# A fourth buffer for the one-hots of a cell group, and building them three groups ahead

## The reference, cut to what matters

```
h = relu(layernorm(x));  x = x + L0(h)   # h @ W1 + b1, then four gated aggregations over the edges
h = relu(layernorm(x));  x = x + L1(h)   # h @ W.T + bias, where W[src, dst] += edge_weight
h = relu(layernorm(x));  x = x + L2(h)   # graph convolution over the edges, normalised by degree
h = relu(layernorm(x));  x = x + L3(h)   # attention over the edges
```

## Time and profile before

| what | us |
|---|---|
| median of 3 runs (lowest, highest) | 993.5 (992.0, 993.78) |
| the profiled execution, its own time | 993.59 |
| span of the profile | 991.7 |
| PE busy | 969.9 (98%) |
| DVE busy | 674.9 (68%) |
| ACT busy | 443.1 (45%) |
| longest time that PE idles between 30 and 118 of the span | 2.30 |

### The profile page before, as it was taken

The page is one execution under the profiler, slowest core; times in us unless marked ns, Lnnn a source line. Parts: engine busy times, 40 slices in busy tenths (PEclk is TensorE's granted clock), DMA queues, the critical chain, the costliest instruction groups (busy, mean ns, idle before and its releaser), DMA issues.

```text
span 991.7 us, 14256 instructions
## 1 busy us (share of the span) xinstructions
PE 969.9 (98%) x5170; PEld 805.5 (81%) x5170; DVE 674.9 (68%) x1223; ACT 443.1 (45%) x662; POOL 140.0 (14%) x191
## 2 busy tenths in 40 slices
PE   5999999999999999999999999999999999999997
PEld 4788878888888888888888888888888888888885
DVE  7887798789788779468874115233346564988886
ACT  5689864544554547223335446002012322445543
POOL 3022510000000001223331000010100000333331
PEclk9999999999999999999999999999999999999999
DMA  7256490000000005543421040732231130101223
GB/s 253 90 187 227 123 272 1 1 22 0 0 21 0 0 0 117 98 147 127 138 96 65 1 171 14 282 113 101 85 128 69 69 122 1 44 22 63 85 85 123
DMA packets 25892, 88.28 MB, mean 89 GB/s; under 512 B 3370, under 2 KB 3370, under 8 KB 25696
## 3 DMA queue, kind: packets, MB, share of 16 engines
q1 hardware_dynamic: 14960, 52.82, 15.1%
q0 software_dynamic: 10880, 34.74, 11.4%
HBM read 59.23 MB, written 33.56 MB: 94 GB/s over the span
## 4 chain that ended last, share of the span: by engine, by line
PE 90%; DVE 5%; ACT 2%; DMA 1%; issue 1%; ACTq 0%; DVEq 0%
PE ps L611 21%; PE ps L2205 11%; PE ps L2179 11%; PE ps L2099 9%; PE ps L2100 9%; PE ps L2101 9%; PE ps L2155 5%; PE ps L2151 5%; PE ps L594 2%; DMA xin<-in_x 1%; PE ps L2022 1%; PE ps L2024 1%; PE ps L2023 1%; PE ps L1949 1%; PE ps L1965 1%
## 5 line engine op out<-in xcount | busy, mean ns | idle before, releaser
L2099 PE MATMUL ps<-g_hi,mask_hi 128*128 128x512 f32 x400 | 157.4, 394 | 2.1 <-DVE mask_lo L1571 2.1
L2101 PE MATMUL ps<-g_hi,mask_lo 128*128 128x512 f32 x400 | 155.8, 390 | 0.0
L2100 PE MATMUL ps<-g_lo,mask_hi 128*128 128x512 f32 x400 | 155.7, 389 | 0.0
L1114 ACT ACTIVATE mask<-ps,v 128x640 f32<-128x640 f32 x80 | 63.5, 793 | 111.3 <-PE ps L2101 52.9
L2205 PE MATMUL ps<-y_all,att_hi 128*128 128x512 f32 x400 | 110.0, 393 | 1.4 <-DVE att_lo L1820 1.4
L2099 PEld LDWEIGHTS ps<-g_hi,mask_hi 128*128 128x128 f32 x400 | 75.1, 188 | 20.5 <-DVE mask_lo L1571 3.3
L2101 PEld LDWEIGHTS ps<-g_hi,mask_lo 128*128 128x128 f32 x400 | 75.1, 188 | 16.0
L2205 PEld LDWEIGHTS ps<-y_all,att_hi 128*128 128x128 f32 x400 | 74.0, 188 | 17.3 <-DVE att_lo L1820 1.6
L2100 PEld LDWEIGHTS ps<-g_lo,mask_hi 128*128 128x128 f32 x400 | 75.1, 188 | 15.0
L611 PE MATMUL ps<-w,hT_hi 128*128 128x512 f32 x320 | 86.6, 392 | 0.0
L577 ACT ACTIVATE hT_hi<-ps 128x1024 fp32r<-128x1024 f32 x30 | 30.8, 1026 | 122.3 <-PE ps L594 122.1
(11 more groups left out here) (221 smaller groups left out, 1932.5 us busy)
## 6 DMA issues: line engine op xcount, KB each, us to landing
xin<-x_after SPq DMA_DIRECT2D x20, 512.0 KB, 3.3
xres<-x_after POOLq DMA_DIRECT2D x20, 512.0 KB, 3.6
x_after<-xres POOLq DMA_DIRECT2D x20, 512.0 KB, 2.9
w_raw<-in_L_gnn_W SPq DMA_DIRECT2D x8, 1024.0 KB, 10.8
x_after<-g POOLq DMA_DIRECT2D x20, 256.0 KB, 7.1
xres<-x_after SPq DMA_DIRECT2D x10, 512.0 KB, 3.3
xin<-in_x SPq DMA_DIRECT2D x9, 512.0 KB, 3.4
out_x<-xres SPq DMA_DIRECT2D x9, 512.0 KB, 2.6
```

The lines of the kernel that those rows point to most:

```text
L1114: nc.scalar.activation(mask[k][:, :], U_ALL, ACT.Tanh, bias=v[:, s:s + 1]).then_inc(tanh_ready, 1)
L2099: nc.tensor.matmul(SUMS[dd], mask_hi[k][:, cols], g_hi[:, s, :], start=(s == 0), stop=False)
L2100: nc.tensor.matmul(SUMS[dd], mask_hi[k][:, cols], g_lo[:, s, :], start=False, stop=False)
L2101: last = nc.tensor.matmul(SUMS[dd], mask_lo[k][:, cols], g_hi[:, s, :], start=False, stop=(s == T - 1))
```

## The change

Two constants change and two tiles are added: `RING` goes from 3 to 4 and `LEAD` from 2 to 3. The fourth pair, `left_last` and `right_last`, lies at 20 and 40 KiB of the region that holds the split first weights, in the gaps in front of `w1_hi` (24 to 40 KiB) and of `w1_lo` (44 to 60 KiB). No other tile moves.

```diff
-RING = 3
+RING = 4
...
-LEAD = 2
+LEAD = 3
...
-    left = [build(f"left{k}", [P, PER_GROUP, P], BF16) for k in range(RING)]
-    right = [build(f"right{k}", [P, PER_GROUP, CELLS + 3 * WCELLS], BF16) for k in range(RING)]
+    left = [build(f"left{k}", [P, PER_GROUP, P], BF16) for k in range(RING - 1)]
+    left += [at("left_last", [P, PER_GROUP, P], BF16, R_Y + 20 * KIB)]
+    right = [build(f"right{k}", [P, PER_GROUP, CELLS + 3 * WCELLS], BF16) for k in range(RING - 1)]
+    right += [at("right_last", [P, PER_GROUP, CELLS + 3 * WCELLS], BF16, R_Y + 40 * KIB)]
```

## The result

The changed kernel takes 994.89 us (median of 11 runs, 994.22 to 996.22), the kernel before 993.5 (11 runs, 992.0 to 994.36). The ratio is 1.0018, 95% interval 1.001 to 1.0026. Timed again beside the kernel before, it takes 995.27 against 993.11, ratio 1.0023 (1.0014 to 1.0032). It is slower by 1.4 to 2.2 us; 2.7 were forecast. One execution of a later experiment, lead1_copies_first, took 5575.49 us for a reason that stays open; it counts in that kernel's median of seven and not in its ratio.

The account below looks back on a forecast made before the run. PE, busy 98%, was taken as the bound, so only its early idle time or clock could matter. 993.59 + 2.65 (1.65 + 1.75 - 0.75) = 996.24, median 0.09 below: 996.2 us; own range 995.4 to 997.0, wider range 994.2 to 998.0.

Parts of the forecast that it names:

- What ends the hole: PE's 2.46 us hole before group 3, tile 2: ended by ACT's late copies of group 2, not by one-hot builds.
- The sum of 2.65: Delay of tile 4's ReLU and PE's group 3: + 1.65 `ew_ids` wait + 1.75 extra build - 0.75 old wait.
- the wait for `ew_ids`: DVE at the start: group 0, now before tile 3's statistics, must wait for `ew_ids`; + 1.65 us.
- the old wait for hT_hi: DVE before hT_lo of tile 2: its former wait for hT_hi disappears; - 0.75 us.
- The steady state: After the start, DVE's waits stay as they are; everything is moved by 2.65 us and nothing shrinks.
- POOL's scale: POOL's six instructions between variance and bias, partly beside group 1's build: 0 to about 1 us on the bias, 0 taken.
- The prediction's last sign: PE's idle time in 31.8 to 50 us grows by about 2.6 us: 1.45 opening, 0.8 group 1 and bias, 0.4 hole.
- The clock: PE's 3.42 us half-clock stretch behind the hole: same single stretch assumed, no difference; could vanish (-1.71) or come twice (+1.71).
- half clock missed after: Rival: most runs after miss PE's half-clock stretch, 993.5 + 2.65 - 1.71 = 994.4 us; chance 0.14.
- The faster rival: PE starves for one-hots before group 3; building further ahead wins 4.17 us, giving 989.3; chance 0.08.

Follow-up runs that it names:

- lead1_copies_first: Kernel before with three places, LEAD 1 instead of 2, and in tile 4 ACT copies group 10 before the ReLU of tile 6 and the bias; 990.21 us, ratio 0.997.
- before_again: The kernel before, unchanged, timed once more with its own trace; 993.19 us, ratio 0.9998.
- after_again: The changed kernel, unchanged, timed once more in the same rounds as the kernel before; 995.27 us, ratio 1.0023.
- lead1: Kernel before with three places and LEAD 1 instead of 2; 990.78 us, ratio 0.9976.
- stats_first: Kernel before (three places, lead two) with the statistics of tile 4 moved in front of the builds of groups 2 and 3 on DVE; 990.21 us, ratio 0.9972.

## Why the prediction was right

**What ends the hole.** Right. The chain builds, statistics, ReLU, bias, copies, group 3 is shown from both sides: one build more in front of the statistics costs 1.76 us, one less gives 1.65, and moving the statistics alone removes the hole with later one-hots.

**The sum of 2.65.** Right: 13.69 - 11.04 = 2.65 in both pairs of traces. Its terms are of another size with another start, though. In the pair with the same start the wait for `ew_ids` is 2.40, not 1.65, and the old wait for hT_hi 1.48, not 0.75. Both end behind the same step on ACT, so their difference holds while each of them moves: 2.40 + 1.75 - 1.48 = 2.67.

**The steady state.** Right: from the opening of tile 3 to the first matmul of the gates (line 2099) PE takes 77.45 us in before_again and 77.36 in after_again.

**POOL's scale.** I left 0 to about 1 us open and took 0. It is the upper end. The bias came 37.03 - 33.45 = 3.58 us after the variance started, against 2.59. POOL's timeline shows where:

```profile
33.69 0.70 POOL L553 TENSOR_TENSOR rough<-variance,minus_half 128x2 f32<-128x2 f32 x1 [17.47 <-DVE variance L533]
34.47 0.19 POOL L555 TENSOR_TENSOR square<-rough 128x2 f32<-128x2 f32 x1
34.74 0.44 POOL L557 TENSOR_TENSOR square<-square,variance 128x2 f32<-128x2 f32 x1
35.27 0.65 POOL L559 TENSOR_SCALAR step<-square 128x2 f32<-128x2 f32 x1
36.00 0.61 POOL L561 TENSOR_TENSOR scale<-rough,step 128x2 f32<-128x2 f32 x1
```

The first two run beside DVE's hT_lo, the next three beside the build that begins at 34.72, and take 0.44, 0.65 and 0.61, where the second took 0.19 and where POOL in the kernel before took 0.20, 0.19 and 0.20 for the same three. That the builds on DVE are what slows POOL is read from this coincidence and not tested. It costs nothing in the end, since group 3 comes later for another reason; but it turns hole into earlier waits. The hole is 1.87 us in the trace after, not 2.88. The prediction's last sign, PE idling about 2.6 us more before tile 3, was too high: the page of stretches gives 3.90 us after, against 1.76 in before_again and 2.30 in the first trace, so 2.14 and 1.60 more. And the growth lies in front of tile 2, the bias and group 1, not in the hole. The steps themselves are 2.64 later; the rest is, by my estimate, how the page counts: a product matmul is busy for 0.39 us where the next can start after 0.23, so each of the three waits more hides some 0.16 us.

**The clock.** This term was mis-sized. I took one stretch at half rate in both kernels, no difference, and judged that most executions pay it. The changed kernel paid it in 0 of 22 runs. The kernel before paid it in its first trace, but only in 24 of the 88 runs that later studies give a clock for. That explains a part of what is missing. In the study of after_again the runs of the kernel before without the stretch have a median of 992.77, and 995.27 - 992.77 = 2.50, near the 2.65; those with it have 993.57. For the first comparison, 1.39 us apart, the clocks of the runs before are not known, so there it stays open. The stretch fell behind holes of 2.46 and 3.66 us, and never in a trace behind one of 1.91 or less. The rival "half clock missed after" came true in its mechanism. Both medians after, 994.89 and 995.27, lie below the forecast's own range of 995.4 to 997.0 and inside the wider one only because that takes in the rivals. The forecast held in its direction and size because only a quarter of the runs before pay the price that its one trace shows; I had not foreseen that, and to this extent it was luck.

The Trainium skill's "TensorE: Matmul & The Clock Gate", Part 1 (The HAM clock gate), says that the same kernel can meet the monitor in another phase from run to run. The runs of one and the same kernel agree in that some pay and some do not: 4 of 11 in before_again. But the length of the hole moves with the start too (2.46 and 1.91 us), and no run here tells the two causes apart.

**The faster rival.** Fell: lead1 and stats_first.

## What to carry to other kernels

A releaser in a trace is only the last of several semaphores that the profile could see. Look whether the tile that it names is the one that this instruction reads, and look at every other condition in the code before a buffer is made deeper or a lead longer.

On an engine that works in order, a longer lead is not free work ahead of time: whatever stands behind the moved work comes later. Ask who waits for that.

When two traces are compared, count from the last step that both have in common, and look in how many runs a stretch at half clock occurs before it goes into a sum.

## What I had not expected of the hardware

The start of the same code moves by 1.9 us (`ew_ids` ends from 28.35 to 30.27), about the spread of each kernel's runs. In all thirteen traces PE waits there for `ew_part`, the parts of the edge weights that POOL prepares, and POOL's last step of it ends between 14.74 and 16.38. One of its small casts takes 0.39 us in the first trace of before and 1.54 in before_again, at nearly the same time and both beside DVE's write of `w_lo`:

```profile
12.77 0.39 POOL L848 CAST ew_part<-ew_rest 80x250 bf16<-80x250 f32 x1
```

```profile
12.69 1.54 POOL L848 CAST ew_part<-ew_rest 80x250 bf16<-80x250 f32 x1
```

Over all traces this cast takes 0.39 to 2.00 us. What decides it was not tested.

PE's pace at the start moves as well. In the first trace of before, the matmuls of tile 0's product follow each other in 0.23 us from the second on. In the trace of after they are still 0.42 to 0.43 us apart up to the one at 22.25:

```profile
20.97 0.63 PE L2025 MATMUL ps<-w_lo,hT_hi 128*128 128x512 f32 x1
21.39 0.63 PE L2026 MATMUL ps<-w_hi,hT_lo 128*128 128x512 f32 x1
21.82 0.63 PE L2024 MATMUL ps<-w_hi,hT_hi 128*128 128x512 f32 x1
22.25 0.45 PE L2025 MATMUL ps<-w_lo,hT_hi 128*128 128x512 f32 x1
22.53 0.40 PE L2026 MATMUL ps<-w_hi,hT_lo 128*128 128x512 f32 x1
```

That is the distance that the same matmuls have in the stretch at 0.50 (45.47 and 45.90 in the trace before). The clock column reads 1.00 here all the same, so that it is the clock is not shown.

A PE that starts late also reaches the hole late (39.94 in the first trace of before, 41.35 in before_again, of which 0.87 is the later `ew_ids`), and the hole hides the rest of the delay. In the traces of the kernel before, the execution with the fast start had the long hole and paid for it with the half clock. If that is the rule, the two partly cancel, which would be why its runs with the half clock are only 0.8 us slower than those without in the study of after_again (0.2 and 1.0 in the two others), and not 1.7; two traces don't show it.
